# Moving the attention sum to a moment matrix of the normed input, with new waits around it

## The reference, cut to what matters

```
xn = layernorm(x)                        # x: 8 x 512 x 128, f32
# branch 1: linear attention, then a gated FFN
q, k, v = split(xn @ Wqkv + bqkv);  qp = elu(q)+1;  kp = elu(k)+1
kv   = einsum('bsd,bse->bde', kp, v)     # per batch, 128 x 128
attn = (qp @ kv) / (qp . sum_s kp + 1e-6)
x1   = layer_norm(xn + attn, g1, b1)
s    = layer_norm(x1 + (silu(x1@Wg+bg) * (x1@Wu+bu)) @ Wd + bd, g2, b2)   # hidden 341
# branch 2: a small net of each token and one of the sequence mean
gf   = sigmoid(net3(mean_s xn))
out  = xn;  3 times: out += coupling(gf, net4(out)) * twist(out)
result = x + s * silu(out)
```

## Time and profile before

| | us |
|---|---|
| median of 3 runs (lowest, highest) | 179.59 (179.36, 179.61) |
| the profiled execution | 179.24 |
| its span, first to last instruction | 177.3 |
| mean granted TensorE clock | 0.981 |
| PE busy, weight loads | 160.2 (90%), 115.7 (65%) |
| DVE, ACT, POOL busy | 147.0 (83%), 122.4 (69%), 108.0 (61%) |

### The profile page before, as it was taken

How to read it: one execution, slowest core, us unless ns; L and a number is a source line. 1 busy time by engine, 2 the same in 40 slices (tenths; PEclk the granted TensorE clock), 3 DMA queues, 4 the chain that set the end, 5 groups by cost and what they waited for, 6 DMA issues and landing times.

```text
span 177.3 us, 3473 instructions
## 1 busy us (share of the span) xinstructions
PE 160.2 (90%) x979; PEld 115.7 (65%) x982; DVE 147.0 (83%) x575; ACT 122.4 (69%) x312; POOL 108.0 (61%) x204
## 2 busy tenths in 40 slices
PE   0389999999999999999999989999999999999920
PEld 0256777777777679545555545788788887888810
DVE  4984879999988987859999996878788989869694
ACT  2238866989989883888888875994677577643530
POOL 0269667969895849940011137379859568595980
PEclk9999999999999996999999999999999999999996
DMA  5890000000000000000000000000001011010113
GB/s 138 253 366 18 0 4 2 0 2 6 0 0 0 0 7 0 0 0 0 4 0 0 6 0 0 2 0 4 2 0 59 4 61 59 0 63 0 59 59 118
DMA packets 3330, 5.74 MB, mean 32 GB/s; under 512 B 496, under 2 KB 1136, under 8 KB 3312
## 3 DMA queue, kind: packets, MB, share of 16 engines
q1 hardware_dynamic: 3312, 5.52, 9.1%
HBM read 3.43 MB, written 2.10 MB: 31 GB/s over the span
## 4 chain that ended last, share of the span: by engine, by line
PE 58%; DVE 19%; POOL 8%; ACT 6%; issue 3%; DMA 2%; SPq 1%; DVEq 0%; ACTq 0%; POOLq 0%
PE bank L1071 11%; PE bank L1059 7%; PE bank L1061 6%; PE bank L1060 6%; DVE r_tok L649 5%; DVE pq L663 5%; PE bank L914 5%; DVE r_tok L652 4%; POOL rstd L240 3%; PE bank L968 3%; PE bank L947 2%; PE bank L948 2%; PE bank L950 2%; DMA r_tok<-in_w_first 2%; PE bank L998 2%
## 5 line engine op out<-in xcount | busy, mean ns | idle before, releaser
L450 ACT ACTIVATE pq<-bank,bffn 128x512 f32<-128x512 f32 (+1 forms) x24 | 16.4, 687 | 17.2 <-PE bank L1061 17.2
L240 POOL TENSOR_TENSOR rstd<-ve,minus_half 128x4 f32<-128x4 f32 (+1 forms) x25 | 24.8, 993 | 2.1
L1071 PE MATMUL bank<-wd,pq 128*128 128x128 f32 x168 | 23.4, 283 | 0.0
L239 POOL TENSOR_SCALAR ve<-mv 128x4 f32<-128x4 f32 (+1 forms) x25 | 5.1, 206 | 29.1 <-DVE nm L549 28.1
L1071 PEld LDWEIGHTS bank<-wd,pq 128*128 128x128 f32 x168 | 21.1, 192 | 0.2
L702 DVE SCALAR_TENSOR_TENSOR pq<-bank,bffn,pq 128x512 f32<-128x512 f32 (+1 forms) x24 | 17.7, 747 | 3.7 <-PE bank L1061 2.7
L1059 PE MATMUL bank<-x_hi,ffn_hi 128*128 128x512 f32 (+1 forms) x48 | 20.4, 424 | 0.0
L401 ACT ACTIVATE q_stage<-bank,col 128x512 f32<-128x512 f32 x24 | 16.4, 687 | 4.8 <-PE bank L914 3.6
L1061 PE MATMUL bank<-x_hi,ffn_lo 128*128 128x512 f32 (+1 forms) x48 | 19.0, 396 | 0.0
L1060 PE MATMUL bank<-x_lo,ffn_hi 128*128 128x512 f32 (+1 forms) x48 | 18.9, 394 | 0.0
L950 PE MATMUL bank<-first_hi,xT_lo 128*128 128x512 f32 x32 | 15.6, 488 | 0.0
(11 more groups left out here) (136 smaller groups left out, 464.3 us busy)
## 6 DMA issues: line engine op xcount, KB each, us to landing
x_tok<-in_x SPq DMA_DIRECT2D x8, 256.0 KB, 6.3
out<-pq SPq DMA_DIRECT2D x7, 256.0 KB, 2.0
r_tok<-in_w_ffn SPq DMA_DIRECT2D x1, 341.0 KB, 7.0
r_tok<-in_w_first SPq DMA_DIRECT2D x1, 320.0 KB, 4.2
out<-pq SPq DMA_DIRECT2D x2, 128.0 KB, 1.8
small<-in_w_small SPq DMA_DIRECT2D x1, 242.0 KB, 3.8
row<-in_rows SPq DMA_DIRECT2D x1, 192.0 KB, 6.6
wd<-in_w_down SPq DMA_DIRECT2D x1, 192.0 KB, 7.1
```

Source lines behind the costliest of these rows:

```text
L240: return pool.tensor_tensor(rstd[i][:, b, ts], ve[i][:, b, ts], minus_half[:, ts], ALU.pow)
L450: act.activation(sg[n % 2][0:m], gate_of(n)[0:m], ACT.Silu, bias=bffn[0:m, c:c + 1]).then_inc(sg_ready, 1)
L1071: last = pe.matmul(dst[:, t * P:(t + 1) * P], hid[b % 2][0:m, c, t * P:(t + 1) * P], wd[0:m, c], start=False, stop=(c == CHUNKS - 1))
```

## The change

- v is no longer computed per token. PE sums a moment matrix M = xnᵀ·[kf, 1] of the normed input with the k features (`sum_m`), ACT copies it (`copy_m`), PE multiplies it once per batch by prepared value weights (`project_kv`), and ACT, not DVE, copies that (`copy_kv`). M's row and column of ones also give the k sum and the sequence mean. `project_tokens` has 384 columns and a bias of 128. M and kv both lie in bank 5.
- `sum_m` of tiles 0 and 1 stands at t = 3 of its batch, behind `project_kv(b-1)`; that of tile 0 waits for `copy_kv(b-1)`. Tiles 2 and 3 follow at t = 0 and 1 of the next batch. `numerator(b-2)` stands behind `project_q(b)`, before tile 0. The rings ek and kf have four buffers.
- The value weights are centred so that u1 has mean zero: `norm_1` has a scale and no bias, and POOL leaves out two small instructions per batch.
- The FFN weights take one ACT and one DVE pass in place of three on DVE. The down bias sits in two spare rows of the last chunk, whose hidden rows are set to 1 by POOL, so the bias products go.
- PE runs 10 and 5 products on ones before it has work. The first weights are loaded from ACT's queue, `eye` by itself, x of batches 1 and 2 ahead of the small weights. DVE's opening is reordered, with `mix_rows` and `value_weights` new.

```diff
 ACT
             def token_tile(n):
                 act.wait_ge(k_ps, n + 1)
-                act.activation(ek[:, n % 3], ps_k[n % 3][:, 0:D], ACT.Exp, ...)
-                act.copy(v1[:, n % 3, 0:D], ps_k[n % 3][:, D:2 * D]).then_inc(v_ready, 1)
-                act.copy(pq[:, n]..., ps_k[n % 3][:, 2 * D:4 * D]).then_inc(pq_ready, 1)
+                act.activation(ek[:, n % KF], ps_k[n % 3][:, 0:D], ACT.Exp, ...)
+                act.copy(pq[:, n]..., ps_k[n % 3][:, D:3 * D]).then_inc(pq_ready, 1)
+            def copy_m(b):
+                act.wait_ge(m_ps, TILES * (b + 1))
+                act.copy(m_sb[:, b], ps_m).then_inc(m_ready, 1)
+            def scale_ffn():
+                act.mul(ffn_hi[:], ffn_raw[:], col[:, COL["g1"]:COL["g1"] + 1]).then_inc(ffn_step, 1)
+            def copy_kv(b):
+                act.wait_ge(kv_ps, b + 1)
+                if b >= 2:
+                    act.wait_ge(num_ps, b - 1)
+                act.copy(kv_sb[:, b % 2], ps_kv).then_inc(kv_ready, 1)
             def norm_1(b, tiles=range(TILES)):
-                    last = act.activation(x1n[...], u1[...], ACT.Identity, scale=rstd[1][...], bias=nmr[1][...])
+                    last = act.mul(x1n[...], u1[...], rstd[1][...])
+            act.dma_start(first_raw[:], w_first).then_inc(first_loaded, 16)
             for b in range(BATCHES):
                 exp_q(b)
                 for t in range(TILES):
                     token_tile(TILES * b + t)
                     if t in (0, 2) and b >= 3:
                         norm_1(b - 3, (t, t + 1))
                     if t == 1 and b + 1 < BATCHES:
                         hi_x(b + 1)
+                    if t == 1 and b >= 1:
+                        copy_m(b - 1)
+                if b >= 1:
+                    copy_kv(b - 1)
                 if b >= 3:
                     hi_x1(b - 3)
+                if b == 1:
+                    scale_ffn()
+            copy_m(BATCHES - 1)
+            copy_kv(BATCHES - 1)
 PE
+            def sum_m(n):
+                b, t = divmod(n, TILES)
+                pe.wait_ge(kf_ready, n + 1)
+                if t == 0 and b >= 1:
+                    pe.wait_ge(kv_ready, b)
+                pe.matmul(ps_m, xn_ext[:, b, t, 1:D + 1], kf[:, n % KF], start=(t == 0), stop=(t == TILES - 1))
+            def mix_weights():         # four f32 products, once, after tile 3
+            def project_kv(b):
+                pe.wait_ge(m_ready, b + 1)
+                pe.matmul(ps_kv, m_sb[:, b, 0:D], wv[:], start=True, stop=True).then_inc(kv_ps, 1)
             for b in range(BATCHES):
                 project_q(b)
+                if b >= 2:
+                    numerator(b - 2)
                 for t in range(TILES):
                     n = TILES * b + t
                     project_tokens(n)
-                    if n >= 2:
-                        sum_kv(n - 2)
+                    if n == TILES - 1:
+                        mix_weights()
+                    if t <= 1 and b >= 1:
+                        sum_m(n - 2)
                     if t == 1 and b + 1 < BATCHES:
                         transpose_x(b + 1)
-                    if t == 3 and b >= 1:
-                        numerator(b - 1)
-                    if t == 3 and b >= 3:
-                        transpose_x1(b - 3)
+                    if t == 3:
+                        if b >= 1:
+                            project_kv(b - 1)
+                        sum_m(n - 3)
+                        sum_m(n - 2)
+                        if b >= 3:
+                            transpose_x1(b - 3)
             down:
-                    pe.matmul(dst[...], ones_bf[:, 0:P], bias3[:, 3 * D:4 * D], start=True, stop=False)
+            warm_up(10) at the outset, warm_up(5) before transpose_x(0)
+            at the end of the loop: sum_m x2, numerator(6), layer_1(0), project_kv(7), global_layer(0),
+            ffn_bias, numerator(7), global_layer(1), layer_1(1), global_layer(2)
 DVE
+            opening: first_lo, bias copy and lo_x(0) ahead of measure(0, 1); mix_rows after it
+            value_weights() once, after tile 3; copy_kv, ctx_sum and two FFN passes are gone
 POOL
+            hid[i][64:P, CHUNKS - 1] set to 1 twice, between scalars_2 and scalars_3
```

More of the change, by code:

```diff
@@ L331, in _ @@
                 scalars_2(j)
+            pool.wait_ge(r_ready, 2 * (PAIRS + 2))
+            for i in range(2):
+                pool.memset(hid[i][64:P, CHUNKS - 1], 1.0).then_inc(hid_ones, 1)
+            pool.wait_ge(hid_ones, 2)
             for j in range(PAIRS):
@@ L351, in hi_x @@
                     act.wait_ge(k_ps, TILES * (b - 1))
[L352 to L353 removed]
+                act.copy(xT_hi[:, b % 2], ps_xT[:]).then_inc(xT_hi_ready, 1)
             def exp_q(b):
@@ L376, in norm_1 @@
                 for t in tiles:
-                    last = act.activation(x1n[:, b % 2, t], u1[:, b % 2, t], ACT.Identity,
-                                          scale=rstd[1][:, b, t:t + 1], bias=nmr[1][:, b, t:t + 1])
+                    last = act.mul(x1n[:, b % 2, t], u1[:, b % 2, t], rstd[1][:, b, t:t + 1])
                 if tiles[-1] == TILES - 1:
@@ L544, in moments, with prepare_rstd @@
                 last.then_inc(mv_ready[i], 1)
-            def negate_mean(i, b, tiles=range(TILES), half=0):
+            def prepare_rstd(i, b, tiles=range(TILES), half=0):
                 dve.wait_ge(mv_ready[i], b + half + 1)
                 ts = slice(tiles[0], tiles[-1] + 1)
-                dve.tensor_scalar(nm[i][:, b, ts], mv[i][:, b, ts, 0], -1.0, None, ALU.mult).then_inc(mean_ready[i], 1)
+                if i == 1:
+                    dve.tensor_scalar(ve[i][:, b, ts], mv[i][:, b, ts, 1], LN_EPS, None, ALU.add).then_inc(mean_ready[i], 1)
+                else:
+                    dve.tensor_scalar(nm[i][:, b, ts], mv[i][:, b, ts, 0], -1.0, None, ALU.mult).then_inc(mean_ready[i], 1)
             def stats(i, b, src):
@@ L774, in split_bias, with mix_rows, value_weights @@
                 last.then_inc(split_ready, 1)
+            def mix_rows():
+                dve.wait_ge(eye_loaded, 16)
+                link(dve.memset(mix, 0.0))
+                link(dve.tensor_copy(mix[:, 0, 0:P - 1], eye[:, 1:P]))
+                dve.memset(mix[0:1, 0, 0:P - 1], -1.0)
+                dve.tensor_copy(mix[:, 1, P - 1:P], col[:, COL["bv"]:COL["bv"] + 1])
+                for i, name in enumerate(("bd", "b1")):
+                    last = dve.tensor_copy(mix[:, 2, CHUNK_ROWS[-1] + i:CHUNK_ROWS[-1] + i + 1],
+                                           col[:, COL[name]:COL[name] + 1])
+                last.then_inc(mix_ready, 1)
+            def value_weights():
+                dve.wait_ge(mix_ps, 1)
+                dve.tensor_copy(gw1[:], ps_w[:, D:D + 64])
+                link(dve.bn_stats(st_v[:], ps_w[:, 0:D]))
+                link(dve.bn_aggr(mv_v[:], st_v[:]))
+                dve.tensor_copy(wv[:, D:D + 1], eye[:, P - 1:P])
+                dve.tensor_scalar(wv[:, 0:D], ps_w[:, 0:D], mv_v[:, 0:1], None, ALU.subtract)
+                dve.wait_ge(down_loaded, 16)
+                dve.tensor_tensor(wd[:, CHUNKS - 1], wd[:, CHUNKS - 1], ps_wd, ALU.add).then_inc(wv_ready, 1)
             dve.memset(minus_one[:], -1.0)
@@ L900, in _ @@
             measure_last(1)
-            negate_mean(2, last, HALVES[0])
+            prepare_rstd(2, last, HALVES[0])
             moments(2, last, HALVES[1], half=1)
-            negate_mean(2, last, HALVES[1], half=1)
+            prepare_rstd(2, last, HALVES[1], half=1)
             for half in range(2):
@@ L915, in transposes, with warm_up @@
                 return last
+            def warm_up(count):
+                for _ in range(count):
+                    pe.matmul(ps_warm, ones_bf[:, 0:P], ones_bf[:], start=True, stop=True)
             def transpose_x(b):
```

223 lines of the change are left out of this document (120 added, 103 removed).

## The result

The changed kernel takes 183.14 us (median of 4 runs, 181.34 to 183.21), before took 179.6 (179.36 to 180.18): a ratio of 1.021, with 95% confidence 1.015 to 1.027. Medians take in every execution, ratios leave out those more than 1.5% above the fastest of their kernel.

The account below looks back on a forecast made before the run. PE was taken as full in the token and FFN stages, with a new PE-ACT ring in the token loop. +0.7 + 3.5 - 0.1 - 1.8 = +2.3 on 179.24 gives 181.5; median 0.35 higher: 181.9 us, range 178.8 to 184.8.

Parts of the forecast that it names:

- The ring: Token loop: PE's sum_m waits for ACT's copy_kv, which waits for PE's tiles; turn 7.83 us against 6.88, +3.5 in all.
- If nothing waited, 6.35: Token loop: without waits a batch would take some 6.35 us, with PE's work at 6.14 and DVE about 6.3.
- no ring: Rival, token loop: the kv copy comes in time, PE waits for nothing, a batch takes 6.35 to 6.15; 175.5 us, chance 0.16.
- The opening: Start up to project_q(2): x 0.4 late, batch 1 transposed at 14.7, project_q(2) at 23.7; +0.7, bounds -0.7 and +2.6.
- 1.2 GHz: Opening: before's first transposes, 1.12 us against 0.60, run at this clock; warmed, they end about 0.7 earlier.
- The clock: Rival: PE, idle in the opening and before numerator(7), runs there at 1.2 GHz; +1.9 and +0.9, 184.7 us, chance 0.15.
- The passage: From project_q(7) to layer 2 of the coupling stage: 14.5 us against 14.64, -0.1, bounds -1.0 and +0.8.
- The FFN: FFN stage: 28 bias products dropped, each holding PE for 0.06 us, -1.8; batches 7.11 us apart.

Follow-up runs that it names:

- the queue's reversal: First weights loaded on the SP queue again, not ACT's, against the changed kernel: 182.17 us, ratio to before 1.021.
- x1n in one piece: ACT's four x1n scalings together behind the first tile, against the kernel with numerator and two sums behind that tile: 177.29 us, ratio 0.976.
- the filled stretch: Eleven more warm-up products before the transposes of x(1), where PE idles, against the changed kernel: 181.28 us, ratio to before 1.010.

## Why the prediction held, step by step

**The ring: right, and the largest term.** PE waits 1.31 in front of `sum_m` for `copy_kv`, as named. The turn is 7.97 against 7.83: ACT 4.21 against 4.25 (half a norm 0.60 for 0.64), PE 3.76 against 3.58. PE's part was too small in three terms: the two sums took 0.52 for 0.44, copy and first sum lie 0.14 apart for 0.04, and from the tile's first product to ACT's exp it is 0.93, only 0.09 less than before's 1.02 and not 0.24 less; transposes and numerator gave 0.15 of it back. In the stream a tile saves 0.17: before, a tile without its sum goes from 46.71 to 47.62 (0.91), now it takes 0.74. That is the three narrower products; the bias half saved nothing. Batch 2's turn was 6.97 for 6.6. Together +4.47 for +3.5. Three orders that leave the instructions alone and open the ring took 5.5 to 6.2 us off the median, and the five turns fell from 38.86 to 34.75, 34.35 and 34.81: shown.

**"If nothing waited, 6.35": half right.** PE's work alone is 6.57 (not 6.14), read where PE never waits, and DVE's turn is 7.26 with 0.97 of stall in it. So "no ring" would not have been 175.5 here: the three kernels came to 176.9 to 177.7. Behind the first ring stand two limits that the prediction did not have: the ring through ACT's second pair of x1n, 7.1 with the stall or without it, and, once that is open, the stall, 7.36 for 6.57. The second is read from four turns of one trace; no run took the stall away with nothing else changed.

**The opening: direction right, size too small.** x was 0.9 late, not 0.4 (shown by the queue's reversal), batch 1 was transposed at 15.41, not 14.7, and q(2) came at 24.52, not 23.7: +1.5 for +0.7 in the profiled execution. Of the 0.8 missed, 0.5 is x. The "1.2 GHz" of before's first transposes rests on their length alone, 1.12 for 0.60; the profile's clock column shows 1.00 there. The Trainium skill (DMA: Bandwidth & Descriptors, section Issuing engines are not separate DMA queues), quoted in the prediction, would have x late; the trace agrees, with 4.42 for 3.54 us.

**The clock: the rival that half came true.** It was put at 0.15 as a fall in the opening (+1.9) and at the passage (+0.9). The fall in the opening stands in nine of the eleven profiles whose idle stretch was left open (not in after's own and not in that of x1n in one piece), and the filled stretch gives 181.28 for 183.14: 1.9, shown. By their times and mean clocks (0.978 and 0.979 against 0.985), three of the four executions of the changed kernel held a case that the forecast had at 0.15. At the passage nothing fell. The price was right; what was wrong was to treat it as one case with the passage, and as unlikely.

**The passage: right in the number, by luck.** -0.27 for -0.1. The 14.5 was the middle between 13.6 at full speed and 15.4 with a fall of the clock. The clock stayed at 1.00 and the passage took 14.37, so the sum at full speed was 0.8 short. Its first part was right, 6.47 for 6.43 to the end of copy_kv(6) (63.38 to 69.85). From there to project_kv(7) at 73.17 it was 3.32 for 3.09, numerator(7) took 1.07 for 0.89 (75.19 to 76.26), layer_1(1) with two steps of the global net 1.49 for 1.2 (76.26 to 77.75).

**The FFN: right in sign, half in size.** -3.5 for -1.8. A batch is 0.54 shorter, so from the first to the seventh `down` it is 40.92 for 44.16, 3.24 less, and the tail gives the other 0.24. Put back, four products cost 0.50: 28 x 0.125 = 3.5. The distance to the next start, 0.06, was taken for the whole price; the rest shows only at the products behind. Shown by putting them back. The f32 products of 128 columns in the same rows, six between 117.53 and the next bias product at 118.26, had the right price, 0.12.

The sum: +0.7 + 3.5 - 0.1 - 1.8 = +2.3 against +1.5 + 4.5 - 0.3 - 3.5 = +2.2. The loop's and the opening's extra 1.8 and the FFN's missing 1.7 cancel; the 181.9 owes its closeness to the profiled 181.34 to that luck. The mechanism, a ring that costs more than the saved products give, was right. The median's distance is the clock. Whether the wait that guards the bank of M and kv could go was not tried.

## What to carry to other kernels

Before adding a wait, follow what is queued behind it on both engines: if each has the other's release behind its own wait, one turn is the sum of both parts, and no busy share of the page shows it beforehand. Place the consumer one step later instead, and look for the next ring: here one stood 0.9 us behind the first. Then ask what is gained at all: with the ring open these turns were no shorter than before's. After moving any instruction ask also what the engines that share memory with it do at that moment, and price a small product by taking it out of a full loop, not by the distance to the next start.

## What the runs showed of the hardware

- TensorE's granted clock fell to 0.50 for some 3 us behind 2.9 to 4.2 us without work in nine of eleven profiles. With eleven products of 0.23 us in the gap it stood at 1.00 in the one profile, and all nine executions stayed between 181.13 and 181.62 us.
- Behind the same warm-up of ten products the next five took 1.25 us in one profile and 2.31 in another, where q(0) started 1.4 later. The column for the clock shows 1.00 in both, so why is open.
- A DVE instruction on 128x4 numbers took 1.14 us, for 0.17, beside a POOL product of 1.28, and 1.13 in another form.
- POOL's tensor_scalar with subtract, its mean read from every second number, took 0.78 us a tile where the form with add took 0.44. Which of the two differences it is stays open.
- A bf16 product of 128 columns cost 0.125 us, an f32 one of 128 columns 0.12, a bf16 one of 512 columns 0.24.
